# A Mamba scan in pairs of channel chunks, with the sum over states by accumulating transposes

## The reference, cut to the two scans

```python
dA = exp(delta[..., None] * A)              # one factor per token, channel and state
dBx = (delta * u)[..., None] * B[:, :, None, :]
state = dA * state + dBx                    # token by token, from zero for each sequence
y = einsum('bdn,bn->bd', state, C)          # sum over the 16 states
y = y + D * u
```

## Time and profile before

| | us |
|---|---|
| median of 3 runs | 3815.44 |
| lowest and highest run | 3812.68, 3817.66 |
| span of the profiled execution | 3813.4 |
| stage BS, from its first piece of `scaled` to its last result | 178.3 |
| block after BS (back to tokens, add to X) | 6.2 |
| stage ES0 | 180.9 |
| stage ES1 | 179.3 |

### The profile page before, as it was taken

How to read it: one execution, slowest core, us unless ns; L and a number is a source line. 1 busy time by engine, 2 the same in 40 slices (tenths; PEclk the granted TensorE clock), 3 DMA queues, 4 the chain that set the end, 5 groups by cost and what they waited for, 6 DMA issues and landing times. The chain is left out here.

```text
span 3813.4 us, 75996 instructions
## 1 busy us (share of the span) xinstructions
PE 3572.9 (94%) x32856; PEld 2539.3 (67%) x32856; DVE 2289.4 (60%) x2561; ACT 1578.1 (41%) x2153; POOL 1281.2 (34%) x792
## 2 busy tenths in 40 slices
PE   7999999999779679999999999999999998797998
PEld 4566666665245555888888888888888846454554
DVE  3677777777269842555555555555555416697972
ACT  2555555555179421222222222222222103697950
POOL 3344444442068321122222222222222004285861
PEclk8999999999779889999999999999999999898999
DMA  6455555553211032111111111111111112111110
GB/s 201 130 146 150 146 151 150 150 141 82 51 55 51 3 155 78 34 50 34 37 44 42 50 42 50 42 50 42 50 42 46 73 42 55 44 52 31 50 45 22
DMA packets 215252, 277.14 MB, mean 73 GB/s; under 512 B 67056, under 2 KB 165328, under 8 KB 213632
## 3 DMA queue, kind: packets, MB, share of 16 engines
q1 hardware_dynamic: 214920, 272.28, 24.6%
HBM read 218.63 MB, written 53.13 MB: 71 GB/s over the span
## 5 line engine op out<-in xcount | busy, mean ns | idle before, releaser
L1806 POOL TENSOR_TENSOR D_ctx_lo<-D_ctx_raw,D_ctx_hi 128x2048 fp32r<-128x2048 f32 (+1 forms) x64 | 269.6, 4213 | 1205.3 <-ACT D_ctx_hi L1800 1205.3
L748 DVE TENSOR_REDUCE A_mxc<-A_psX 128x2 f32<-128x768 f32 (+2 forms) x512 | 480.9, 984 | 113.8 <-PE A_psX L790 109.9
L1065 ACT ACTIVATE A_probs<-A_psE 128x1024 f32<-128x1024 f32 (+1 forms) x416 | 426.7, 1026 | 294.3 <-PE A_psE L1123 292.2
L1825 ACT ACTIVATE D_V<-D_psY 128x384 f32<-128x384 f32 x208 | 102.2, 491 | 890.2 <-PE D_psY L1891 890.2
L1841 DVE TENSOR_REDUCE D_mxc<-D_psE 128x4 f32<-128x1536 f32 (+2 forms) x128 | 241.9, 1890 | 204.2 <-PE D_psE L1919 204.2
L2182 ACT ACTIVATE D_probs<-D_psE 128x2048 f32<-128x2048 f32 x112 | 210.5, 1880 | 295.8 <-PE D_psE L2295 295.8
L330 POOL TENSOR_TENSOR ES_hcp<-E_du,E_Cn 128x512 f32<-128x512 f32 x224 | 285.3, 1278 | 128.3 <-DVE E_du L357 98.4
L2311 PE MATMUL D_psO<-D_probs,D_V 128*32 128x256 f32 (+1 forms) x5376 | 313.3, 381 | 0.0
L1891 PE MATMUL D_psY<-D_wv_hi,D_ctx_hi 128*128 128x384 f32 x832 | 285.5, 343 | 0.0
L1881 PE MATMUL D_psY<-D_ctx_hi,D_wk_hi 128*128 128x384 f32 (+2 forms) x768 | 279.8, 364 | 0.7 <-POOL D_ctx_lo L1806 0.7
L1891 PE MATMUL D_psY<-D_wv_hi,D_ctx_lo 128*128 128x384 f32 x832 | 279.1, 335 | 0.0
(11 more groups left out here) (372 smaller groups left out, 7864.0 us busy)
## 6 DMA issues: line engine op xcount, KB each, us to landing
A_land<-in_ctx SPq DMA_DIRECT2D x32, 768.0 KB, 5.7
D_ctx_raw<-in_ctx SPq DMA_DIRECT2D x32, 768.0 KB, 4.7
A_land<-in_ctx SPq DMA_DIRECT2D x16, 1024.0 KB, 6.0
D_ctx_raw<-in_ctx SPq DMA_DIRECT2D x16, 1024.0 KB, 5.9
E_Cn<-bc_scratch SPq DMA_DIRECT2D x64, 256.0 KB, 3.3
k_scratch<-A_Khl SPq DMA_DIRECT2D x32, 384.0 KB, 4.4
A_Kst<-k_scratch SPq DMA_DIRECT2D x64, 192.0 KB, 3.7
A_land<-in_ctx SPq DMA_DIRECT2D x16, 642.0 KB, 4.3
```

What stands on the lines that cost most here:

```text
L748: nc.vector.tensor_reduce(mxc[:, u % 4, :, u // 4], psX[:, x % 2, :, 0:w], axis=AX_X, op=ALU.max).then_inc(x_free, 1)
L1065: nc.scalar.activation(probs[0:KW[k], n % NPR, :, :].rearrange("p h q -> p (h q)"), psE[0:KW[k], :], ACT.Exp, scale=HD ** -0.5).then_inc(e ...
L1806: nc.gpsimd.tensor_tensor(ctx_lo[c][:, :, 0:w], ctx_raw[c][:, :, 0:w], ctx_hi[c][:, :, 0:w].bitcast(F32), ALU.subtract).then_inc(lo_done[c ...
```

## The change

`scan_states` is rewritten, and the block after BS is removed.

- A step now covers two chunks (W = 2): a call has 64 pair steps. One scan runs over 128x1024, one POOL multiplication over 128x1024 with the row of C broadcast over both chunks. All products with C are on POOL; DVE has none.
- `h` and the product `hc` lie in the tile `du`, two buffers each (NH = NP = 2); `dB` has two buffers of two PSUM banks (NE = 2).
- For even states B is applied as before. For odd states ACT scales only the identity, 128x128, to a diagonal of B, and PE multiplies `duT` with it: an fp32 matmul of 128 moving columns in the place of each transpose.
- The sum over states is made by transposes that accumulate in `acc`, four of 128x128 for each chunk; `acc` then holds tokens on partitions.
- D * u is made in place by POOL at the start of a call (four instructions of 128x1024) and added by PE as one more part of the last state's sum.
- First layer: DVE adds `acc` to X within the scan. Second layer (`gate`): ACT copies `acc` to `yt`, PE transposes it back (`turn_back`), DVE multiplies with the gate.

```diff
-        NH, NP, ND, NE = 2, 4, 3, 3
+        NH, NP, ND, NE, NS = 2, 2, 3, 2, 3
+        W = 2
+        CP = CN // W
...
+        h = du[:, 0:2, :].rearrange("p k (w t) -> p k w t", w=W)
+        hc = du[:, 2:4, :].rearrange("p k (w t) -> p k w t", w=W)
...
+        def piece(m, i):
+            t = TILES * (m // N_STATE) + i
+            if diagonal(m):
+                return scaled[:, m % NS, i, 0:P], consts["ident"][:, :], b_col(t, m % N_STATE)
+            return scaled[:, m % NS, i, :], duT[:, t, :], b_col(t, m % N_STATE)
...
             def _(pool):
+                for c in range(CN):
+                    nc.gpsimd.tensor_scalar(skip[:, c, :], skip[:, c, :], skip_col(c), None, ALU.mult
+                                            ).then_inc(skip_ready, 1)
+                for s, (half, n, cp) in enumerate(STEPS):
...
                     pool.wait_ge(h_ready, s + 1)
+                    if s >= NP:
+                        pool.wait_ge(summed, s - NP + 1)
...
+                    nc.gpsimd.tensor_tensor(hc[:, s % NP], h[:, s % NH],
+                                            rows.C[:, q % NR, :].unsqueeze(1).broadcast_to([P, W, HALF]), ALU.mult
+                                            ).then_inc(hc_ready, 1)
...
                 def scan(s):
+                    dve.wait_ge(da_ready, W * (s + 1))
+                    dve.wait_ge(db_full, s + 1)
+                    if s >= NH:
+                        dve.wait_ge(hc_ready, s - NH + 1)
...
+                def entering(s):
...
                     pe.wait_ge(scaled_ready, TILES * (m + 1))
+                    if s >= NE:
+                        pe.wait_ge(h_ready, s - NE + 1)
+                    for j, c in enumerate(chunks(s)):
+                        for i in range(TILES):
+                            to = dB[:, s % NE, j, bass.ts(i, P)]
+                            if diagonal(m):
+                                last = nc.tensor.matmul(to, duT[:, TILES * half + i, bass.ts(c, P)], scaled[:, m % NS, i, 0:P],
+                                                        start=True, stop=True)
+                            else:
+                                last = nc.tensor.transpose(to, scaled[:, m % NS, i, bass.ts(c, P)], consts["ident"][:, :])
...
                 def add(s):
+                    pe.wait_ge(hc_ready, s + 1)
...
+                        for part in parts:
+                            for i in range(TILES):
+                                last = nc.tensor.matmul(acc[:, c, bass.ts(i, P)], part[:, bass.ts(i, P)],
+                                                        consts["ident"][:, :], start=(n == 0 and i == 0),
+                                                        stop=(n == N_STATE - 1), is_transpose=True,
+                                                        skip_group_check=True)
+                    last.then_inc(summed, 1)
...
+                for s in range(len(STEPS) + 1):
+                    if s + NE < len(STEPS):
+                        entering(s + NE)
+                    if s:
+                        add(s - 1)
+                    if gate is not None and s - 2 in nth_last:
+                        turn_back(s - 2)
```

More of the change, by code:

```diff
@@ L243, in scan_states @@
[L243 to L268, removed]
@@ L274, in tokens, with chunks @@
+        def chunks(s):
+            return range(W * STEPS[s][2], W * STEPS[s][2] + W)
         def tokens(tile, c, half):
@@ L292, in times_b @@
                 def times_b(m, i):
[L293 to L299, removed]
+                    if m >= NS and i == 0:
+                        act.wait_ge(db_full, CP * (m - NS + 1))
@@ L300, in _ @@
                 ahead = 0
-                for m, i in pieces[:TILES]:
-                    times_b(m, i)
+                for p in PIECES[:TILES]:
+                    times_b(*p)
                     ahead += 1
                 act.wait_ge(cleared, 1)
-                for s, (half, n, c) in enumerate(STEPS):
+                for s, (half, n, cp) in enumerate(STEPS):
                     if s >= ND:
                         act.wait_ge(h_ready, s - ND + 1)
[L308 to L312, removed]
-                        ahead += 1
+                    for j, c in enumerate(chunks(s)):
+                        nc.scalar.activation(dA[:, s % ND, j, :].rearrange("p (b t) -> p b t", t=S)[:, :, 1:S],
+                                             tokens(delta, c, half).rearrange("p (b t) -> p b t", t=S)[:, :, 1:S],
+                                             ACT.Exp, scale=A[:, c, n:n + 1]).then_inc(da_ready, 1)
+                    for p in [p for p in PIECES[ahead:] if TILES * p[0] + p[1] < (2 * TILES, 11, 14, 8 + W * s)[min(s, 3)]]:
+                        times_b(*p)
+                        ahead += 1
+                    if gate is not None and s - 3 in nth_last:
+                        copy_out(s - 3)
@@ L315, in _ @@
+                for s in LASTS:
+                    if gate is not None and s + 3 >= len(STEPS):
+                        copy_out(s)
             @block.gpsimd
             def _(pool):
[L317 to L321, removed]
@@ L360, in times_c @@
[L360 to L368, removed]
@@ L370, in finish @@
-                def finish(s):
[L371 to L378, removed]
@@ new lines, in add, with turn_back @@
+                    last.then_inc(summed, 1)
+                def turn_back(s):
+                    for j, c in enumerate(chunks(s)):
+                        pe.wait_ge(copied, W * nth_last[s] + j + 1)
+                        for i in range(TILES):
+                            last = nc.tensor.transpose(acc[:, c, bass.ts(i, P)], yt[:, j, bass.ts(i, P)],
+                                                       consts["ident"][:, :])
+                        last.then_inc(turned, 1)
+                for s in range(NE):
+                    entering(s)
@@ L426, in scan_states @@
+                for s in range(len(STEPS) + 1):
[5 more added lines that the diff above has]
+                        turn_back(s - 2)
+                for s in LASTS:
+                    if gate is not None and s + 2 >= len(STEPS) + 1:
+                        turn_back(s)
         r.restart()
```

160 lines of the change are left out of this document (60 added, 100 removed).

## The result

The changed kernel takes 3829.74 us (median; 3826.26 to 3838.03), the kernel before 3814.69 us on the same chip: a ratio of 1.0044, 95% interval [1.0031, 1.0057], 15 us slower. The forecast was 3818.5 in a range of 3798 to 3844. The time lies in the range, but the likeliest case, a difference within 0.2%, did not come: it is slower by 0.4%.

The account below looks back on a forecast made before the run. It took a loop of waits through scan, PE and POOL to bind, 10.51 us against 10.38; stages +1.3, +3.2 and +4.8, less the 6.2 block, made +3.1 on 3815.4, so 3818.5 us, range 3798 to 3844.

Parts of the forecast that it names:

- the likeliest case: Whole kernel: time within 0.2% (7.6 us) of before, 3808 to 3823; chance 0.42.
- loop of waits: Steady part of a stage: scan, PE's queued inputs and sums, POOL's product; 10.51 us for four pair steps against 10.38 now.
- the scan: DVE, each pair step: one scan of 1024 takes 2.28 us, bounds 2.2 and twice 1.21.
- POOL's 1024: POOL, each pair step: one product of 1024 with C takes 2.35 us.
- the accumulating transpose: PE's sums: one instruction at 0.110 us, eight in 0.88 us; chance 0.03 that it is two instructions, giving 3902 us.
- the clock: PE in the steady stretch: granted clock 1.00; rival that transposes don't keep it up, 77 us more, chance 0.04.
- the tails: Stage end, from the last scan's start: 8.2 us in BS, 10.5 us with the gate.
- The block of 6.20: The block after BS, 6.20 us, goes wholly.
- POOL's start: Stage start: POOL's four products with D at 1.04 us each, ending before the first h; upper bound 2.35 each, +7 us.
- mid-stage: Middle of a stage, where the last state's sums carry D * u: 0.7 us more, 2.9 with the gate.
- the low clock: First states of a stage, where PE's clock falls and rises: 0 to 2.5 us a stage, taken as 0.5.
- the rival of the odd products: PE's odd inputs: 32 loop instructions at 0.118 us each, 10.77 us a period, 3830 us; chance 0.22.

Follow-up runs that it names:

- e6: Changed kernel with a third buffer for the product hc, two still for h: 3791.05 us, ratio 0.9932 to the kernel before.
- e2: Changed kernel with a third buffer for h, one product buffer moved to its own tile: 3770.97 us, ratio 0.9889 to the kernel before.
- e1: Changed kernel with the four products with D moved from POOL's start to ACT at steps 6 to 9: 3820.66 us, ratio 1.0019 to the kernel before.
- e8: Changed kernel with POOL's four products with D written as products of two tensors, D's column broadcast: 3818.29 us, one run.
- e4: Changed kernel with odd states' inputs by transposes too, no diagonal products: 3791.93 us, ratio 0.9949 to the kernel before.

## Why the prediction came out as it did

**Right: the mechanism.** PE's saving comes back as latency in a loop of waits over scan, odd inputs, sums and POOL. The term was 10.51 us for four pair steps; it is 10.62 to 10.63, with each link where the forecast put it, and it goes to 9.74 or 9.39 when a buffer cuts it (e6, e2). Right too are the scan, POOL's 1024, the accumulating transpose (eight in 0.88 us, 0.110 apart), the clock, and the tails: 8.17 (8.2) in BS and 10.42 (10.5) in ES. The block of 6.20 went.

**Wrong: POOL's start.** The step that failed is "POOL's four products with D at the start: 1.04 us each if they cost what a copy does, 2.35 if what a two-input product does", taken at the first "since they read one tensor". They cost 2.846, above the upper bound: a tensor times a column as scalar was bounded by two operations that resemble it in what they read, and neither is its form. With that bound the term would have been up to 2.5 a stage; e1 gives 2.2 to 3.1, 8.3 in all, and e8 10.4, part of it an earlier clock in one stage. Without it (e1) the ratio is 1.0019, on the edge of "within 0.2%" with an interval of [1.0010, 1.0029]: this step is the largest that made the kernel slower, but whether it alone did is not shown. That the time lies in the range all the same owes something to luck: the range had 7 us for POOL's start at a price that was too low.

By terms, for the three stages together: from the stage's start to the first scan +0.6; the pace +4.7 (63 steps of 0.025); between first and last scan, beyond the pace, 19.4 us where 8.0 were forecast (0.7 and twice 2.9 at mid-stage, three times 0.5 for the clock), so +11.4; the tails -0.2. Sum +16.5, the difference between 19.5 and 3.1 but for rounding. Of the +11.4, mid-stage is 1.1 (its four gaps are 1.0 us over a period in BS and 3.3 in each ES), and the rest, 10.3, lies nearly all at the starts: POOL's 8.3, with the two late fifth gaps in it, and the low clock.

**Mis-sized: the low clock.** 0.5 us a stage was set down. With POOL out of the way (e1) the second gap is 4.08 us in place of 2.53, and the first four gaps together are still 1.2 to 1.4 us over a period. The diagonal products at this clock fit that: 16 of them, 0.213 us apart in place of 0.112, take 1.6 us more, and the forecast had no term for them. Where the clock rose before them (second stage of e8) the gap is 3.00. The 0.5 was also to cover a clock that falls and rises in the first states; in each ES stage of the changed kernel, where it fell again after PE had waited for POOL, that alone is 1.2 to 1.4 us.

**Half right: the rival of the odd products.** Its 3830 is almost the measured time, but not for its reason. It put all 32 odd instructions at 0.118; the two groups in the loop take (1.85 + 1.79) / 32 = 0.1138, just past the point from which the rival was to decide (0.1135; by the forecast's own sum 3823 is passed at 0.113). That is the 0.12 of the loop, some 5 us of the 16.5. But one product follows the other after 0.112, near the 0.110 of the scaling by columns; the other 0.07 us is the first one after a wait, whose next follows after 0.185.

**Not explained.** The stages are 19.5 us longer and the medians 15 us apart. Outside the stages the changed kernel and its variants took 24.3 to 25.2 us between ES0 and ES1 and 118.8 to 121.1 after ES1; the one trace of before has 26.14 and 122.3. That would be 2 to 5 us in the changed code's favour, but with one trace of before, and no run made for it, the cause stays open. The differences between single executions are larger: ahead of BS, in code that the change leaves as it was, the ten traces took 1080.7 to 1093.7 us, the changed kernel's the longest.

## What to carry to other kernels

Where an engine's work is cut, follow the longest way through the waits over the buffers before counting the saving: here PE went from busy for 96% of a stage (BS) to 85% and the pace stayed, and one more buffer of 128x1024 turned 0.4% slower into 1.1% faster. Reordering one engine's queue only moved the wait. Price an instruction by a row of its own form, and where there is none set the bounds wider than two relatives make them, above all for what runs at the start of a stage, where nothing covers it.

## What the runs showed of the hardware that was not expected

- POOL, 128x1024 fp32: times a column as scalar 2.846 us, times the same column as a broadcast second tensor 1.895, times a broadcast row (the products with C) 2.37. On ACT the scaled copy takes 1.134.
- In the start of BS the granted clock was 0.50 up to about 1105, though PE had worked since 1096.30 with one idle stretch of 0.84 us. In ES0 it was 1.00 while PE was busy for 5.30 of 10.10 us, and 0.50 right behind that. In the steady part it was 1.00 with transposes alone (e4) as well as in the changed kernel (1131 to 1273), which has the diagonal products.
- Diagonal products start 0.112 us apart at the full clock and 0.213 at the lower one, where the transposes are 0.213 apart too. After a wait the second starts 0.185 us behind the first, so that 16 take 1.85 us in place of 1.79.
